# Attention layers: three PSUM banks for projections, one for contexts, and each pair's normalising one third of a sample later

## The reference

```
q, k, v = heads(x @ Wq + bq), heads(x @ Wk + bk), heads(x @ Wv + bv)
probs   = softmax(q @ k.T / 8 + where(adj, 0, -9e15))
x       = layernorm(x + (probs @ v) @ Wf + bf)
```

## Time and profile before

| | |
|---|---|
| median of three runs | 3392.78 us |
| profiled execution: time, span | 3394.71 us, 3392.9 us |
| PE (matmul) busy | 3138.5 us, 93% |
| DVE busy | 2426.2 us, 72% |
| ACT busy | 2060.1 us, 61% |
| POOL busy | 1055.9 us, 31% |
| granted TensorE clock, mean | 0.993 |

### The profile page before, as it was taken

How to read it: one execution, slowest core, us unless ns; L and a number is a source line. 1 busy time by engine, 2 the same in 40 slices (tenths; PEclk the granted TensorE clock), 3 DMA queues, 4 the chain that set the end, 5 groups by cost and what they waited for, 6 DMA issues and landing times. The chain is left out here.

```text
span 3392.9 us, 80994 instructions
## 1 busy us (share of the span) xinstructions
PE 3138.5 (93%) x24736; PEld 2633.6 (78%) x24736; DVE 2426.2 (72%) x8331; ACT 2060.1 (61%) x6315; POOL 1055.9 (31%) x1014
## 2 busy tenths in 40 slices
PE   6999999999995999999999999999999999999997
PEld 5777777777774788878888788878888888878886
DVE  4767767767774777777777777777777777777776
ACT  5878788878884555555555555555555555555554
POOL 1333333333333423232322423232323223232323
PEclk9999999999997999999999999999999999999999
DMA  2011001101102111111111111111111011111110
GB/s 71 23 31 32 27 27 32 32 22 32 32 16 72 31 32 42 32 43 31 42 35 38 60 41 37 36 38 36 42 32 42 32 42 37 36 38 36 42 32 30
DMA packets 107121, 123.91 MB, mean 37 GB/s; under 512 B 39680, under 2 KB 106176, under 8 KB 106176
## 3 DMA queue, kind: packets, MB, share of 16 engines
q1 hardware_dynamic: 106688, 118.57, 11.1%
HBM read 68.22 MB, written 50.33 MB: 35 GB/s over the span
## 5 line engine op out<-in xcount | busy, mean ns | idle before, releaser
L835 ACT ACTIVATE a_probs<-a_logits,a_nmax 128x256 f32<-128x256 f32 x1152 | 574.0, 502 | 273.9 <-DVE a_nmax L916 273.9
L774 POOL TENSOR_TENSOR a_residual<-a_x,a_br 128x384 f32<-128x384 f32 x192 | 191.1, 1019 | 1542.1 <-DVE a_mix L944 1528.4
L96 PE MATMUL a_pj<-a_xt_hi,a_w_lo 128*128 128x256 f32 x1728 | 512.7, 297 | 6.1 <-DVE a_xt_lo L901 5.2
L97 PE MATMUL a_pj<-a_xt_lo,a_w_hi 128*128 128x256 f32 x1728 | 484.2, 280 | 0.0
L98 PE MATMUL a_pj<-a_xt_hi,a_w_hi 128*128 128x256 f32 x1728 | 483.9, 280 | 0.0
L466 DVE CUSTOM_DVE_ANT_0 g_v<-g_z,g_v 128x256 f32<-128x256 f32 x768 | 293.3, 419 | 245.3 <-ACT g_v L364 242.4
L916 DVE CUSTOM_DVE_ANT_0 a_logits<-a_s,a_mask 128x256 f32<-128x256 f32 x1152 | 416.6, 417 | 0.8 <-PE a_s L1070 0.5
L937 DVE TENSOR_SCALAR a_probs<-a_probs,a_recs 128x256 f32<-128x256 f32 x1152 | 395.0, 385 | 20.4
L370 ACT ACTIVATE g_exps<-g_v,g_nmax 128x256 f32<-128x256 f32 x768 | 383.9, 509 | 0.9 <-DVE g_nmax L466 0.7
L96 PEld LDWEIGHTS a_pj<-a_xt_hi,a_w_lo 128*128 128x128 f32 x1728 | 325.4, 188 | 33.4 <-issue 5.4
L906 DVE SCALAR_TENSOR_TENSOR a_qk_lo<-a_pj,a_bc,a_qk_hi 128x256 fp32r<-128x256 f32 x576 | 251.1, 477 | 131.0 <-ACT a_qk_hi L828 131.0
(11 more groups left out here) (116 smaller groups left out, 8360.8 us busy)
## 6 DMA issues: line engine op xcount, KB each, us to landing
a_x<-y SPq DMA_DIRECT2D x96, 384.0 KB, 3.1
y<-a_out SPq DMA_DIRECT2D x96, 384.0 KB, 2.5
g_x<-x SPq DMA_DIRECT2D x32, 384.0 KB, 3.0
y<-g_out SPq DMA_DIRECT2D x32, 384.0 KB, 2.5
w_stage<-att_w SPq DMA_DIRECT2D x3, 2304.0 KB, 9.8
a_adj<-adj SPq DMA_DIRECT2D x96, 64.0 KB, 2.8
g_adj<-adj SPq DMA_DIRECT2D x32, 64.0 KB, 2.8
g_w_stage<-gat_w SPq DMA_DIRECT2D x1, 1152.0 KB, 5.6
```

The source lines that it names most:

```text
L96: pe.matmul(out, a[1], b[0], start=first, stop=False)
L97: pe.matmul(out, a[0], b[1], start=False, stop=False)
L835: last = act.activation(probs[:, (HEADS * u + h) % 4, t, :], logits[:, h % 2, t, :], ACT.Exp, scale=-1.0, bias=nmax[:, u, h, t:t + 1], acc ...
```

## The change

`pj_ps` gets a third bank and `cx_ps` gives one up. The nine results of a unit go over the three banks in turn, always the same ones. The waits that guard a bank move accordingly. In the three `slot` functions, `normalise` of pair 0 moves from the first third to the second, that of pair 1 from the second to the last, and that of pair 2 from the last third to the first third of the next slot, where it stands for `prev`, with the transposing of x's low part between its two heads. Both exponentials of a pair now stand ahead of `high_qk`. With one bank, each context pair waits for `low_ct` of the pair before. No instruction is added or removed but waits.

```diff
-        cx_ps = [ctx.enter_context(nc.psum_tensor(f"a_cx{i}", [P, 512], F32)) for i in range(2)]
-        pj_ps = [ctx.enter_context(nc.psum_tensor(f"a_pj{i}", [P, 512], F32)) for i in range(2)]
+        cx_ps = ctx.enter_context(nc.psum_tensor("a_cx", [P, 512], F32))
+        pj_ps = [ctx.enter_context(nc.psum_tensor(f"a_pj{i}", [P, 512], F32)) for i in range(3)]
...
-            return pj_ps[(u + BANK_ORDER.index(what)) % 2]
+            return pj_ps[BANK_ORDER.index(what) % 3]
...                                                   (ACT, slot)
                 if nxt:
                     high_xt(*nxt, 0)
                     high_xt(*nxt, 1)
+                if prev:
+                    high_ct(*prev, 1, prev_layer)
+                    even_pt(*prev, 2)
                 if cur:
                     exp(*cur, 0)
-                if prev:
-                    even_pt(*prev, 2)
+                    exp(*cur, 1)
                 if nxt:
                     high_qk(*nxt, 0, nxt_layer)
-                if cur:
-                    exp(*cur, 1)
-                if prev:
-                    high_ct(*prev, 1, prev_layer)
-                if nxt:
                     copy_v(*nxt, 0)
 
                 if cur:
                     exp(*cur, 2)
+                    exp(*cur, 3)
                 if nxt:
                     high_qk(*nxt, 1, nxt_layer)
-                if cur:
-                    exp(*cur, 3)
+                if prev:
+                    high_ct(*prev, 2, prev_layer)
+                if cur:
                     even_pt(*cur, 0)
-                if prev:
-                    high_ct(*prev, 2, prev_layer)
                 if nxt:
                     copy_v(*nxt, 1)
 
                 if cur:
                     exp(*cur, 4)
+                    exp(*cur, 5)
                 if nxt:
                     high_qk(*nxt, 2, nxt_layer)
                 if cur:
-                    exp(*cur, 5)
                     high_ct(*cur, 0, cur_layer)
                     even_pt(*cur, 1)
...                                                   (DVE, slot)
+                if prev:
+                    normalise(*prev, 4)
                 if nxt:
                     low_xt(*nxt, 0)
                     low_xt(*nxt, 1)
+                if prev:
+                    normalise(*prev, 5)
                 if cur:
                     mask_and_max(*cur, 0)
                     mask_and_max(*cur, 1)
                 if prev:
                     odd_pt(*prev, 2)
+                if nxt:
+                    low_qk(*nxt, 0, nxt_layer)
+                if prev:
+                    low_ct(*prev, 1, prev_layer)
+
                 if cur:
                     normalise(*cur, 0)
-                if nxt:
-                    low_qk(*nxt, 0, nxt_layer)
-                if cur:
                     normalise(*cur, 1)
-                if prev:
-                    low_ct(*prev, 1, prev_layer)
-
-                if cur:
                     mask_and_max(*cur, 2)
                     mask_and_max(*cur, 3)
+                if nxt:
+                    low_qk(*nxt, 1, nxt_layer)
+                if cur:
+                    odd_pt(*cur, 0)
+                if prev:
+                    low_ct(*prev, 2, prev_layer)
+
+                if cur:
                     normalise(*cur, 2)
-                if nxt:
-                    low_qk(*nxt, 1, nxt_layer)
-                if cur:
-                    odd_pt(*cur, 0)
                     normalise(*cur, 3)
-                if prev:
-                    low_ct(*prev, 2, prev_layer)
-
-                if cur:
                     mask_and_max(*cur, 4)
                     mask_and_max(*cur, 5)
-                    normalise(*cur, 4)
                 if nxt:
                     low_qk(*nxt, 2, nxt_layer)
                 if prev:
                     add_back(*prev, 0)
-                if cur:
-                    normalise(*cur, 5)
-                if prev:
                     add_back(*prev, 1)
                     statistics(*prev)
                 if cur:
+                    low_ct(*cur, 0, cur_layer)
                     odd_pt(*cur, 1)
-                    low_ct(*cur, 0, cur_layer)
...                                                   (PE)
-            def transpose_x(half, u, t, opening):
-                if opening:
-                    pe.wait_ge(v_read, at(NT, half, u, 0))
+            def transpose_x(half, u, t):
+                if t == 0:
                     pe.wait_ge(pj_read, at(HI_STEPS, half, u, 0))
-                pe.wait_ge(back_read, at(NT, half, u, t + 1 - 3 * NT))
-                if t == 0:
                     pe.wait_ge(x_loaded[u], half * 32 + 32)
+                else:
+                    pe.wait_ge(back_read, at(NT, half, u, 1 - 3 * NT))
...
-                pe.wait_ge(pj_read, split_of(half, u, X[1] if chunk == 0 else QK[chunk - 1]))
+                    pe.wait_ge(back_read, at(NT, half, u, -2 * NT))
+                    pe.wait_ge(pj_read, split_of(half, u, X[1]))
+                elif chunk == 2:
+                    pe.wait_ge(v_read, at(NT, half, u, 1))
...                                                   (make_v, t == 1)
-                    pe.wait_ge(v_read, at(NT, half, u, 1))
+                    pe.wait_ge(pj_read, split_of(half, u, QK[0]))
...                                                   (make_back)
                 if nxt and t == 0:
+                    pe.wait_ge(pj_read, split_of(*nxt, QK[1]))
+                elif nxt:
                     pe.wait_ge(v_read, at(NT, *nxt, NT))
-                elif nxt:
-                    pe.wait_ge(pj_read, split_of(*nxt, QK[2]))
...                                                   (pair_of_contexts)
-                pe.wait_ge(ct_split, at(DC, half, u, c - 1))
+                pe.wait_ge(ct_split, at(DC, half, u, c))
```

More of the change, by code:

```diff
@@ L683, in split_of, with bank @@
             return at(HI_STEPS, half, u, (X + QK).index(k) + 1)
-        def bank(u, what):
-            return pj_ps[(u + BANK_ORDER.index(what)) % 2]
+        def bank(what):
+            return pj_ps[BANK_ORDER.index(what) % 3]
         def evictions(half, u, h):
@@ L818, in copy_v @@
                 act.wait_ge(contexts, at(DC, half, u, -DC))
[L819 removed]
+                act.activation(v_sb[u][:, t, :], bank(f"v{t}")[:, 0:D], ACT.Identity).then_inc(v_read, 1)
             def high_xt(half, u, t):
                 act.wait_ge(pj_made, step(half, u, X[t]))
[L823 removed]
+                act.activation(xt_hi[:, :, t * P:(t + 1) * P], bank(f"x{t}")[:, 0:D].rearrange("p (c n) -> p c n", c=DC), ACT.Identity).then_inc(pj_hi, 1)
             def high_qk(half, u, c, layer):
@@ L827, in high_qk @@
                 for m in (Q, K):
-                    last = act.activation(qk_hi[u][:, c, m, :], bank(u, f"qk{c}")[:, m * N:(m + 1) * N], ACT.Identity, bias=bc[:, layer, m, c:c + 1])
+                    last = act.activation(qk_hi[u][:, c, m, :], bank(f"qk{c}")[:, m * N:(m + 1) * N], ACT.Identity, bias=bc[:, layer, m, c:c + 1])
                 last.then_inc(pj_hi, 1)
@@ L905, in low_qk @@
                 for m in (Q, K):
-                    last = dve.scalar_tensor_tensor(qk_lo[u][:, c, m, :], bank(u, f"qk{c}")[:, m * N:(m + 1) * N], bc[:, layer, m, c:c + 1],
+                    last = dve.scalar_tensor_tensor(qk_lo[u][:, c, m, :], bank(f"qk{c}")[:, m * N:(m + 1) * N], bc[:, layer, m, c:c + 1],
                                                     f32(qk_hi[u][:, c, m, :]), ALU.add, ALU.subtract)
@@ L943, in add_back @@
                 dve.wait_ge(back_made, at(NT, half, u, t + 1))
-                dve.tensor_tensor(mix[:, t, :], bank(u, f"back{t}")[:, 0:D], residual[u][:, t, :], ALU.add).then_inc(back_read, 1)
+                dve.tensor_tensor(mix[:, t, :], bank(f"back{t}")[:, 0:D], residual[u][:, t, :], ALU.add).then_inc(back_read, 1)
             def statistics(half, u):
@@ L973, in slot @@
                 if cur:
+                    normalise(*cur, 0)
+                    normalise(*cur, 1)
                     mask_and_max(*cur, 2)
                     mask_and_max(*cur, 3)
-                    normalise(*cur, 2)
                 if nxt:
@@ L985, in slot @@
                 if cur:
+                    normalise(*cur, 2)
+                    normalise(*cur, 3)
                     mask_and_max(*cur, 4)
                     mask_and_max(*cur, 5)
-                    normalise(*cur, 4)
                 if nxt:
@@ L1029, in make_qk @@
                     for c in range(DC):
-                        last = product(pe, bank(u, f"qk{chunk}")[:, m * N:(m + 1) * N], (hi[:, m, c, cols], lo[:, m, c, cols]), (xt_hi[:, c, :], xt_lo[:, c, :]),
+                        last = product(pe, bank(f"qk{chunk}")[:, m * N:(m + 1) * N], (hi[:, m, c, cols], lo[:, m, c, cols]), (xt_hi[:, c, :], xt_lo[:, c, :]),
                                        first=c == 0, last=c == DC - 1)
@@ L1039, in make_v @@
                 for c in range(DC):
```

(14 more changed lines are left out.)

17 lines of the change are left out of this document (8 added, 9 removed).

## The result

The changed kernel takes 3543.22 us (median of 4 runs, 3539.07 to 3547.49), the kernel before 3395.6 (4 runs): ratio 1.0437, 95% interval 1.0416 to 1.0457. That is 148 us slower, where the forecast was 339 us slower; the time lies inside the range of 3520 to 3785. It is 12 us from the 3531 of the rival in which POOL doesn't hold `normalise` 5 up, which had a chance of 0.13.

A forecast was written before the change was run, and what follows sets the result against it. PE was taken as the bound, busy 22.79 of a 23.78 us slot. The new loop's 27.39 us slot adds 3.61 us, times 94 is 339 us, giving 3732 us; forecast 3680 to 3785, full range 3520 to 3785.

The forecast's parts named there:

- the rival in which POOL doesn't hold `normalise` 5 up: In the attention slot, `normalise` 5 runs through undisturbed by POOL: slot 25.25 us, time 3531 us; chance 0.13.
- The banks: On PE, the second `make_back` no longer waits for `low_qk` 2: gain of 1.1 us a slot, 103 us.
- The loop: From PE's third context pair through `copy_v` 0, ACT and DVE to `normalise` 5 and back: 25.25 us undisturbed, before 23.78.
- When `normalise` 5 ends: On DVE, its multiplications meet POOL's first `layer_norm` instruction and end after the second, at 19.88, not 17.74: period 27.39 us.
- That the context bank and the other waits cost nothing: On PE, `low_ct` ends before the next context pair needs the single bank; other waits add under 0.1 us.
- That the granted clock costs nothing: In the attention slots, a granted PE clock below 1.00 was counted as no cost.
- The rival that the bank was the bound and nothing takes its place: In the attention slots, removing PE's wait in `make_back` gives its full gain: 3290 us; chance of faster 0.08.
- The rule of a whole instruction: On DVE and POOL, two-port instructions lock each other out for a whole instruction; by it the period is 27.39 us.

The follow-up runs named there:

- e1: The changed kernel with the ACT and DVE orders of the kernel before, so only banks and their waits change: 3281.32 us, ratio 0.9664.
- e3: The changed kernel with `copy_v` 0 moved on ACT from ahead of `exp` 2 to between `exp` 3 and `high_qk` 1: 3404.01 us, ratio 1.0021.
- e8: The changed kernel with the DVE order of the kernel before, ACT's order and the banks as changed: 3452.93 us, ratio 1.0183.
- e2: The kernel before with the ACT and DVE orders of the changed kernel, banks as before: 3866.77 us, ratio 1.1382.
- e5: The changed kernel with POOL's two `layer_norm` instructions in the attention layers replaced by additions of 384 columns, for timing alone: 3589.0 us, ratio 1.0582.
- e6: The changed kernel with the two scalar pointers of `layer_norm` replaced by constants, for timing alone: 3537.23 us, ratio 1.0433.
- e10: The changed kernel with two more DVE `bn_stats` instructions of 256 columns directly ahead of `normalise` 5: 3627.24 us, ratio 1.0692.

## Why the prediction was wrong in size

- *The banks.* Right: 103 us forecast, 114 measured alone (e1); and the wait in `make_back` is gone after the change.
- *The loop.* Right, step by step to within 0.1 us, and its hinge, `copy_v` 0 on PE's contexts, is shown by e3 (3404 us). It costs 25.25 a slot undisturbed by the forecast, 25.23 measured.
- *When `normalise` 5 ends.* This step failed: "So a multiplication that meets a running POOL instruction waits for its end". The term was 2.14 us a slot, 201 us; it measured 0. I took the price from the row at 1139.53, where POOL ran an addition and a cast, and carried it to an instruction of another kind. The row nearer in kind was the one at 2024.08, with the same `layer_norm` instruction, and I read it wrongly as bearing the rule out. It is a pair. By the rule its first multiplication would have waited for POOL's end at 2024.92 and the second would have ended about 0.3 us behind it, so the row would be some 1.25 us long and not 0.98. The trace of the kernel before has the two apart (ns: shortest, median, longest):

```profile
L937 DVE TENSOR_SCALAR a_probs<-a_probs,a_recs x2: 356/532/709, 2024.1 to 2024.4; 128x256 f32<-128x256 f32 x2
```

The first, 0.8 us after POOL's start, ran through in 0.356 us; only the second, at 1.1, was held. The same happens in some 80 slots of that kernel. So the row spoke against a block of the whole instruction, and for a free part that includes 0.8. It didn't show that 0.5, where `normalise` 5 falls, is free too; the profile after does.
- *That the context bank and the other waits cost nothing.* Right here and in e1. It isn't so under every order: in e8 PE waits for it once a slot.
- *That the granted clock costs nothing.* Right in the typical slot (1.00 in the one shown), not over the whole run (0.988 instead of 0.993). In e2 it made up the whole miss.
- *The rival that the bank was the bound and nothing takes its place.* Its number, 3290, is what e1 gives; for the change itself it was wrong, because the change also moved the order. The Trainium skill, Perfetto Trace Analysis, section Optimization Strategy, holds that the same gap repeating on the engine that should be saturated can mean too little SBUF or PSUM. The trace of e1 agrees: with the new banks and the old order the gap is gone, and the kernel is 3.4% faster.
- *The rule of a whole instruction.* The Trainium skill, SBUF — State Buffer, section Who interferes with whom, has whoever issues first take the shared ports for its whole instruction. The traces agree for POOL's additions of 384 (e5) and 1152 columns and its casts of 1152, and not for its `tensor_scalar` of 384 float32 columns (0.35 us for a multiplication inside its 1.65), where the measurement decides.

## What to carry to other kernels

Where in-order engines hand work to each other in turn, walk the loop from one wait back to itself over a period, with distances from a timeline; the stages in it that another engine used to cover now count in full. In such a queue look for an instruction whose wait is unrelated to what stands behind it: here one `copy_v` of 0.5 us in the wrong place cost 139 us. Where a row shows several instructions under one length, take them apart before you read a rule from it. A change of two parts wants each alone: here the banks were worth 3.4%, and the order turned that into a loss.

## What the runs showed of the hardware

A `tensor_scalar` of POOL on 384 float32 columns takes 1.65 us (1.49 with constants, e6), and it holds a DVE multiplication in SBUF off only in parts of that. These are the meetings in the traces of the ten kernels that have it as it stands, by the time from its start at which the multiplication was issued:

- Up to 0.1 us (109, most of them in e10): nearly all took 0.35 us, and POOL's instruction took 1.78 instead of 1.65.
- 0.2 to 0.45 us (130): they ended at about 0.8.
- 0.5 to 1.05 us (1151): all but three took 0.35 us.
- 1.1 to 1.3 us (251): all ended 0.15 us after POOL's end, with 0.63 us in e10.

Why it is in two parts is open. POOL's additions of 384 and 1152 columns and casts of 1152 held multiplications off to their end (up to 2.7 us). Its `inverse_std` instruction of 2 columns, 0.83 us long, didn't: multiplications issued inside it took 0.35.
